# Identity products ahead of TensorE's waits in a gated cross-attention and mixture-of-experts kernel

## What is computed

```python
x = x + tanh(g_xattn[0]) * xattn(layernorm(x), ctx_1024, mask, Wq, Wk, Wv, Wo)
x = x + tanh(g_ffn[0])   * ffn(layernorm(x), ...)

# xattn: 16 query heads, 8 key/value heads of 128, keys and values from 361 context rows
# ffn:
h = rms(x) * w_ln1
q, k, v = h @ wq + bq, h @ wk + bk, h @ wv + bv         # 16 heads of 32, then rope on q and k
x = x + softmax(causal(q @ k.T * 32 ** -0.5)) @ v @ wo
h = rms(x) * w_ln2
probs = softmax(h @ w_router)                           # 8 experts, the best 2 of each token
routed = sum over the 2 of  w * (silu(h @ w_gate_e) * (h @ w_up_e)) @ w_down_e   # inner width 352
sh = (silu(h @ w_sh_gate) * (h @ w_sh_up)) @ w_sh_down * sigmoid(h @ w_sh_eg)    # inner width 1408
x = x + routed + sh
```

## Time and profile before

| | |
|---|---|
| median of 3 runs | 961.73 us (960.95 to 968.34) |
| the profiled execution's own time | 965.36 us |
| its span, first to last instruction | 963.6 us |
| mean granted TensorE clock over the span | 0.974 |
| PE busy | 901.0 us (94%) |
| PE weight loads | 836.1 us (87%) |
| DVE busy | 638.6 us (66%) |
| ACT busy | 561.1 us (58%) |
| POOL busy | 399.7 us (41%) |
| DMA | 122.20 MB, 127 GB/s on average |

### The profile page before, as it was taken

How to read it: one execution, slowest core, us unless ns; L and a number is a source line. 1 busy time by engine, 2 the same in 40 slices (tenths; PEclk the granted TensorE clock), 3 DMA queues, 4 the chain that set the end, 5 groups by cost and what they waited for, 6 DMA issues and landing times.

```text
span 963.6 us, 16195 instructions
## 1 busy us (share of the span) xinstructions
PE 901.0 (94%) x5743; PEld 836.1 (87%) x5743; DVE 638.6 (66%) x1442; ACT 561.1 (58%) x1448; POOL 399.7 (41%) x384
## 2 busy tenths in 40 slices
PE   5999999999999999999989998799979999999997
PEld 4889999999999999999867767699979888988897
DVE  3557777743537777762486976575867778987764
ACT  3656666754546666663334767545446767776761
POOL 3432222345442223246534433344233766666531
PEclk9999999999999999999998899699999989999999
DMA  5734710016540000005431112134376989999876
GB/s 149 215 87 121 205 52 2 12 41 170 156 123 1 17 1 2 1 12 153 135 92 55 45 35 66 39 96 127 95 267 194 288 239 294 287 307 270 269 198 156
DMA packets 112760, 122.20 MB, mean 127 GB/s; under 512 B 9887, under 2 KB 77927, under 8 KB 112680
## 3 DMA queue, kind: packets, MB, share of 16 engines
q1 hardware_dynamic: 97806, 98.80, 33.2%
q0 software_dynamic: 5184, 12.13, 6.1%
q10 hardware_dynamic: 9690, 10.24, 3.7%
HBM read 110.72 MB, written 19.07 MB: 135 GB/s over the span
## 4 chain that ended last, share of the span: by engine, by line
PE 65%; DVE 14%; DMA 11%; ACT 4%; issue 4%; POOL 1%; ACTq 0%; SPq 0%; DVEq 0%; POOLq 0%
PE bank L2080 59%; PE bank L2209 4%; DVE we L1348 3%; DMA s_sum<-yo,target 2%; DMA eraw<-in_L_ffn_w_up_e_dram 2%; DMA eraw<-in_L_ffn_w_gate_e_dram 2%; DMA eraw<-in_L_ffn_w_down_e_dram 2%; DVE wf L1348 1%; DMA sums<-s_sum 1%; ACT we L921 1%; DMA raw<-in_L_xattn_Wq_dram 1%; DVE PQ L1345 1%; PE bank L2386 1%; POOL wx L1918 1%; DVE HDl L1348 1%
## 5 line engine op out<-in xcount | busy, mean ns | idle before, releaser
L1947 POOL TENSOR_SCALAR SC<-SC,mx,anyv 100x361 f32<-100x361 f32 x128 | 81.4, 647 | 211.5 <-DVE mx L1460 200.9
L1918 POOL TENSOR_TENSOR wf<-raw,wf 128x512 fp32r<-128x512 f32 x54 | 71.6, 1332 | 107.7 <-ACT wf L907 107.7
L1918 POOL TENSOR_TENSOR wx<-raw,wx 128x512 fp32r<-128x512 f32 x64 | 83.9, 1320 | 74.4 <-ACT wx L907 74.2
L921 ACT ACTIVATE we<-eraw 128x704 fp32r<-128x704 f32 (+2 forms) x140 | 96.1, 718 | 28.5 <-DMA eraw<-in_L_ffn_w_up_e_dram 8.8
L1348 DVE TENSOR_TENSOR we<-eraw,we 128x704 fp32r<-128x704 f32 (+2 forms) x100 | 92.2, 941 | 24.2 <-ACT we L921 23.9
L1930 POOL TENSOR_TENSOR we<-eraw,we 128x704 fp32r<-128x704 f32 x40 | 72.8, 1821 | 67.9 <-ACT we L921 67.7
L2080 PE MATMUL bank<-H2h,wf 128*128 128x400 f32 x352 | 99.0, 347 | 0.0
L1037 ACT ACTIVATE SC<-SC,mx 100x361 f32<-100x361 f32 x128 | 75.4, 593 | 29.1 <-DVE mx L1456 28.6
L2080 PE MATMUL bank<-XTh,wx 128*128 128x400 f32 x256 | 72.0, 354 | 3.3 <-POOL wx L1918 2.0
L1348 DVE TENSOR_TENSOR Kl<-bank,Kh 128x362 fp32r<-128x362 f32 x64 | 34.1, 534 | 60.3 <-ACT Kh L995 60.2
L1348 DVE TENSOR_TENSOR QOl<-bank,QOh 128x200 fp32r<-128x200 f32 (+1 forms) x96 | 41.4, 432 | 45.4 <-ACT QOh L950 35.4
(11 more groups left out here) (288 smaller groups left out, 2770.9 us busy)
## 6 DMA issues: line engine op xcount, KB each, us to landing
raw<-s_unit SPq DMA_DIRECT2D x60, 256.0 KB
eraw<-in_L_ffn_w_gate_e_dram SPq DMA_DIRECT2D x40, 352.0 KB
eraw<-in_L_ffn_w_up_e_dram SPq DMA_DIRECT2D x40, 352.0 KB
eraw<-in_L_ffn_w_down_e_dram SPq DMA_DIRECT2D x40, 256.0 KB
raw<-in_L_xattn_Wq_dram SPq DMA_DIRECT2D x32, 256.0 KB
raw<-in_L_xattn_Wo_dram SPq DMA_DIRECT2D x32, 256.0 KB
eraw<-in_L_ffn_w_down_e_dram SPq DMA_DIRECT2D x20, 192.0 KB
s_unit<-in_L_ffn_w_sh_gate_dram SPq DMA_DIRECT2D x11, 256.0 KB, 3.9
```

The lines of the kernel that those rows point to most:

```text
L921: eng.activation(weights("e", u)[0:rows, 0, 0:n], eraw[u % 6][0:rows, 0:n], ACT.Copy).then_inc(sem("act_e"), 1)
L1918: eng.tensor_tensor(w[:, 1, :, :], raw[plan.raw[stream, u] % 4][:, :, :], f32(w[:, 0, :, :]), ALU.subtract).then_inc(sem("pool_w"), 1)
L1947: eng.tensor_scalar(sc, sc, m[:, 3, h:h + 1], anyv[:, b:b + 1], ALU.mult, ALU.mult).then_inc(sem("pool_p"), 1)
```

## The change

A helper `keep_warm(bank, n)` issues `n` products of the 128x128 identity with itself into the first 128 columns of a bank that is free at that point; nothing reads them, and the bank's next user starts with a product that overwrites. They are placed, by two tables, at these points of PE's program, 146 products in all:
- 12 products of zeros (`Z`) before everything else, once POOL has cleared `Z`; 3 behind the first sequence's `x_turn`; 4 ahead of `q_tile(0, 0)`;
- 5 ahead of `qk(0, 0)`, 4 ahead of each of the first two products with `swap`, 7 ahead of `v_row(0)`, 4 ahead of the first scores;
- 35 at ten points of self-attention (`WARM_RING`), and 8 more: 2 ahead of the transpose of job 3, 3 ahead of `po(0, 0)`, 3 ahead of `elog(0)`;
- 3 ahead of `eg` of each of the 20 routed blocks.

In `self_attention` the wait for the scaled probabilities (`plan.scaled`) now stands behind the waits for the bank, so that the products come between them. In `po` the bank is asked for ahead of the weights. A few waits are repeated earlier (`act_yt`, `dve_x1`) so that the bank of the products is free.

```diff
+WARM = {"head": 12, ("x_turn", 0, 1): 3, ("q", 0, 0): 4, "qk": 5, "swap": 4, "vrow": 7, "scores": 4, ("turn", 3): 2, ("po", 0, 0): 3,
+        ("elog", 0): 3, "block": 3}
+
+WARM_RING = {("scores", 2, 0): (4, ("qk", 1, 5)), ("turn", 9): (3, ("vbat", 0)), ("scores", 5, 0): (5, ("po", 0, 0)),
+             ("turn", 21): (3, ("er", 0, 1)), ("scores", 7, 0): (2, ("er", 0, 3)), ("out", 5): (3, ("eh", 0, 0)),
+             ("turn", 25): (6, ("eh", 0, 0)), ("out", 6): (3, ("eh", 0, 3)), ("turn", 29): (2, ("elog", 0)),
+             ("out", 7): (4, ("esoft", 0))}
...
+        def keep_warm(bank, n):
+
+            for _ in range(n):
+                mm(bank[:, 0:128], ident[:, :], ident[:, :], True, True)
+
+        def warm_ring(*key):
+
+            if key in WARM_RING:
+                n, later = WARM_RING[key]
+                keep_warm(free_bank(later), n)
+
+        def warm_up():
+
+            pe.wait_ge(sem("pool_const"), CONST["zero"])
+            for _ in range(WARM["head"]):
+                mm(banks[0][:, 0:128], Z[:, HB, 0:128], Z[:, HB, 128:256], True, True)
+
         def x_turn(half, i):
             n = half * HB + i
+            keep_warm(banks[0], WARM.get(("x_turn", half, i), 0))
...
         def q_tile(half, n):
+            keep_warm(banks[n % 4], WARM.get(("q", half, n), 0))
...
         def qk(h, n):
+            if (h, n) == (0, 0):
+                pe.wait_ge(sem("act_yt"), KD + (n - 2) % 4 + 1)
+                keep_warm(banks[0], WARM["qk"])
...
         def swap_halves(n):
 
+            if n < 2:
+                pe.wait_ge(sem("act_yt"), 2 * KD)
+                keep_warm(banks[n + 2], WARM["swap"])
...
         def v_row(k):
+            if k == 0:
+                pe.wait_ge(sem("dve_x1"), B - 1)
+                keep_warm(banks[6], WARM["vrow"])
...
             strips = (2 * pair, 2 * pair + 1)
+            if (q, pair) == (0, 0):
+                pe.wait_ge(sem("dve_x1"), B - 1)
+                keep_warm(banks[6], WARM["scores"])
+            warm_ring("scores", q, pair)
...
             h, b = divmod(q, HB)
+            warm_ring("out", q)
             pe.wait_ge(sem("act_ft"), 2 * q + 2)
...
             if 0 <= u < 32:
-                name, value = plan.scaled(u)
-                pe.wait_ge(sem(name), value)
+                warm_ring("turn", u)
...
+                keep_warm(banks[3 + u % 2], WARM.get(("turn", u), 0))
+                name, value = plan.scaled(u)
+                pe.wait_ge(sem(name), value)
...
         def po(h, m):
+            bank = free_bank(("po", h, m))
+            keep_warm(bank, WARM.get(("po", h, m), 0))
             w = unit("f")
             pe.wait_ge(sem("dve_cx"), HB * (h + 1))
-            bank = free_bank(("po", h, m))
...
             bank = free_bank(("elog", h))
+            keep_warm(bank, WARM.get(("elog", h), 0))
...
             bank = free_bank((name, i))
+            if name == "eg":
+                keep_warm(bank, WARM["block"])
             pe.wait_ge(sem("dve_xe"), i + 1)
...
+        warm_up()
         pe.wait_ge(sem("pool_const"), CONST["pad"])
```

## The result

| | before | after |
|---|---|---|
| median | 961.56 us (4 runs, 960.95 to 968.34) | 950.61 us (4 runs, 950.11 to 952.15) |
| ratio | | 0.9884, 95% interval 0.9838 to 0.9931 |
| profiled execution | 965.36 us, span 963.6, clock 0.974 | 952.15 us, span 950.3, clock 0.993 |

What follows compares the result with a forecast made beforehand. PE, busy 94% of the span, was taken to bound the kernel. Terms 1.2 - 0.3 + 3.0 + 0.3 + 3.6 + 1.0 = 8.8 us off the 961.73 us median gave 952.9 us, own range 949 to 957, overall 945 to 965.

Steps and rivals of the forecast that it cites:

- What a product costs: Every added product on PE: 0.22 us by columns; 0.38 us if it waits for both weight loads.
- third rival: Routed blocks: PE sets every block's pace, products paid in full; 960.9 us at 0.22 each, 970.5 at 0.38; chance 0.20.
- Head: Kernel start, 19 products in PE's waits: 1.2 us won, ends 0 and 1.8; 0 if transposes don't count as busy.
- `qk`, `swap`, `v_row`: Products where the clock is already up: nothing comes back in this execution, 0.3 us lost, ends 0 and 1.0.
- First scores: 4 products in the wait for `HTl` keep 513.5 to 520.5 us at full clock: 3.0 us won, ends 0 and 3.4.
- Around job 3: 537.5 to 544.5 us stays at full clock, but DVE is busy 6.84 of 7: 0.3 us won, ends 0 and 1.
- Jobs 9 to 29, `po`, `elog`: Late self-attention: products fill waits of 0.5 to 2 us; 3.6 us won, ends 2.0 and 5.5.
- the slow stretch then goes: Late self-attention, 605.5 to 623 us: with the waits filled, the half-clock stretch disappears; 2.35 and 1.25 us come back.
- Routed stage: 60 products ahead of routed blocks: 4.3 us won, 3.3 paid, together 1.0 won; ends 5.4 won and 3.3 lost.
- The second rival: Whole kernel: the clock falls all the same, nothing is won; between 962 and 965.3 us, middle 963; chance 0.20.
- The first: Whole kernel: all of it comes back, every upper end reached, 16.8 us won, 944.9 us; chance 0.18.

Runs made afterwards that it cites:

- e1_none: Changed kernel with every product count set to 0, its moved and added waits kept: 963.28 us, ratio 0.9999 to the kernel before.
- e6_head_no_zeros: Changed kernel with only the head's 3 and 4 identity products, without the 12 of zeros and all others: 964.3 us, ratio 1.0022 to the kernel before.
- e7: Changed kernel without the 20 products at qk, swap and v_row: 954.5 us, ratio 0.9898 to the kernel before.
- e11: Changed kernel with 16 products ahead of the first routed block, 2 ahead of the others, 2 more at jobs 26, 27, 28 each: 950.34 us, ratio 0.9829.
- e12: Changed kernel with 16 products ahead of the first routed block, 1 ahead of the others, 2 more at jobs 26, 27, 28 each: 949.85 us, ratio 0.9839.
- e5: Changed kernel with 6 products ahead of each routed block instead of 3: 959.79 us, ratio 0.9961 to the kernel before.
- e4_head_only: Changed kernel with only the 19 products of the head, zeros included: 960.89 us, ratio 0.9958 to the kernel before.

## Why the prediction was right

The time lies 2.3 us below the forecast and within its own range of 949 to 957. The mechanism is the one that was forecast: `e1_none` gives none of the gain, and the clock is up behind nearly all of the products. The sum of 8.8 us was put together from the places of one trace, though, and holds better as a sum than place by place. Over all traces the parts come out as 2.7 us for the head, 6.3 for self-attention (6.9 forecast) and 1.4 for the routed blocks (1.0 forecast), less 0.1 at `swap`: 10.3, where 10.7 and 11.0 were timed. What was mis-sized is mainly the head, 1.2 for 2.7. By its steps, in the pair of traces:

- **What a product costs**: 0.22 us by columns was taken, the rows show 0.22 (0.89 us for four). The other end, 0.38 us for two open weight loads, is refuted; with it goes most of the third rival.
- **Head**: 1.2 us, measured 2.9 in this pair and about 2.7 over all traces. The mechanism is right and the term too small: what is won by 21 us (some 1.5) isn't all, and by the first key tile more has come, which I put down to PE getting the following weights sooner; no run tests that. The prediction also gave the time with this term at 0. The Trainium skill, "TensorE: Matmul & The Clock Gate", section "Part 4: PE-mode transpose", says that transposes don't count as a busy PE; no run here tests that, but the term of 0 that I drew from it is wrong: the first key tile starts earlier in each of the ten traces with products in the head than in any without, in `e6_head_no_zeros`, with the seven alone, by 1.7 us.
- **`qk`, `swap`, `v_row`**: 0.3 us lost, measured 0.15 (2.93 to 2.79). PE is 0.89 us late at the first `swap` and 1.6 after the second and has caught up by 486 us, as argued; at `v_row` it is 1.8 us late and has caught up by 501. But "nothing comes back in this execution" is all that could be said: e1 and e7 have falls near 470 and e6 one at 500.6, each worth about 1.5 us.
- **First scores**: 3.0 us, measured 3.05. The size of the fall was read rightly, but that it stood in both the forecast and the pair is one draw: of the five traces without products there, two have it. The forecast has nothing for the place near 575 us, where four of the five lose 2.5 to 4.0 us and the trace of before nothing.
- **Around job 3**: 0.3 us, measured 0.85; that DVE, busy 6.84 us of 7, held the rest back is argued, not tested.
- **Jobs 9 to 29, `po`, `elog`**: 3.6 us, measured 2.1. The step that failed is "the slow stretch then goes": it shrank (0.91 in its window, not 1.00), because short waits for DVE and POOL stand between jobs 26 and 28, where no product is. With six more products there it is gone in both traces (e11, e12).
- **Routed stage**: 1.0 us, measured 5.4 in this pair, less 0.7 behind it. The size is off because the trace of before had one of the longer stages (198.6 us, the six without the products average 196.4) and that of after one of the shorter. Over the traces it is 2.1 less 0.7, near the forecast, and timed it can't be told from nothing. That waits swallow a part of the products and the rest is paid is what e5 shows (6.9 of 13.3 us paid, no wait left); how much of the first 13.2 is paid no run gives. The fall at the first block got no term: the prediction reads falls as coming behind a microsecond or two of idle time and not one long wait, but the one at 721.7 us starts within a wait of 4.9, and 16 products there (e11, e12) removed it.

The third rival's mechanism is real but it doesn't hold for every block: with three products ten of the 19 distances between blocks are 9.56 us, and some blocks still wait (3.1 us in all); with six none does. The second rival, that the clock falls all the same, was wrong. The first, that all comes back (944.9), was not reached; with the falls at the first block and at jobs 26 to 28 filled too, e12 came to 949.85 us, 0.9839. The forecast said last that the falls might stand elsewhere in the next execution, and e1 shows it.

## What to carry to other kernels

Where an engine slows down after idle time, cheap work ahead of its waits can give back what the slow stretches cost, if that engine is what the rest waits for (self-attention, 6.3 us; in the routed stage hardly anything). Its price is zero up to the length of the wait and full beyond it, as six products a block show; so count it in start-to-start time, and fit it to each wait rather than give every block the same. Read the places from several executions: the falls of one trace are a draw, and a place that was never slow in it (`qk`) may be so in the next. A part whose worth is below the spread of single runs is better read as the time between two of the engine's own instructions, over all traces, than from the medians.

## What the runs showed of the hardware that was not expected

- The same program has its falls of the clock at different places in different executions (471, 536, 577 and 608 us in e1; 513, 537 and 605 before), with waits in the same places. How much they take differs too: the mean clock of 82 runs of the kernel before lies between 0.966 and 0.986.
- Products of zeros can wake the clock: behind 12 of them four transposes took 0.54 us instead of 0.90 in `e4_head_only`, and 0.54 or 0.55 in six of the nine traces that have them.
- The page's clock line reads 9 and the windows read 1.00 in the head, where rows of 0.54 and 0.67 us show the lower clock (15 to 18 us in the trace of before, for one); only the timeline tells of the slow start.
